# A recommender tower on one core: four slots for the vectors, lookups of chunk 1 ahead of the products of chunk 0, and each step of products in two visits

## The reference

```
e = jnp.stack([tbl_0[ids[:, 0]], tbl_1[ids[:, 1]],
...
combined = jnp.concatenate([dense_features[:, None, :], sparse_features], axis=1)
interactions = jnp.einsum('bnd,bmd->bnm', combined, combined)
interactions_flat = interactions[:, _TRIU_I, _TRIU_J]
...
h = jnp.concatenate([z, r_dense_features], axis=1)
h = jnp.maximum(h @ W_top1 + b_top1, 0.0)
h = jnp.maximum(h @ W_top2 + b_top2, 0.0)
y = h @ W_top3
```

## Time and profile before

| what | value |
|---|---|
| time, median of 3 runs | 372.38 us (370.5 to 372.94) |
| profiled execution, span from first to last instruction | 373.1 us |
| TensorE busy | 332.0 us (89%) |
| GpSimd busy | 258.6 us (69%) |
| VectorE busy, ScalarE busy | 207.1 us, 188.8 us |
| granted TensorE clock, mean | 0.977 |

### The profile page before, as it was taken

How to read it: one execution, slowest core, us unless ns; L and a number is a source line. 1 busy time by engine, 2 the same in 40 slices (tenths; PEclk the granted TensorE clock), 3 DMA queues, 4 the chain that set the end, 5 groups by cost and what they waited for, 6 DMA issues and landing times.

```text
span 373.1 us, 13491 instructions
## 1 busy us (share of the span) xinstructions
PE 332.0 (89%) x6048; PEld 298.5 (80%) x6048; DVE 207.1 (55%) x375; ACT 188.8 (51%) x223; POOL 258.6 (69%) x280
## 2 busy tenths in 40 slices
PE   0377859899999899998999999999999999999895
PEld 0377848898799778996789978998799878997685
DVE  3799745694089703874059912885079704860030
ACT  2698462455545473553635564554645563556402
POOL 6777777777777777777777777777777777776000
PEclk9997898899999999998999999999999999999999
DMA  7999426772226622464215722464226622442230
GB/s 178 246 259 212 135 79 174 193 229 69 55 68 151 198 53 59 95 194 125 58 54 128 233 54 58 93 192 131 58 59 150 205 54 57 105 116 62 51 40 21
DMA packets 49332, 44.24 MB, mean 119 GB/s; under 512 B 33359, under 2 KB 39094, under 8 KB 49274
## 3 DMA queue, kind: packets, MB, share of 16 engines
q1 hardware_dynamic: 39166, 25.36, 26.9%
q0 software_dynamic: 8704, 17.84, 18.2%
q10 hardware_dynamic: 1404, 0.17, 0.3%
HBM read 37.91 MB, written 5.44 MB: 116 GB/s over the span
## 4 chain that ended last, share of the span: by engine, by line
PE 82%; DMA 5%; issue 5%; ACT 4%; DVE 2%; SPq 1%; ACTq 1%; DVEq 0%
PE banks L443 38%; PE banks L462 14%; PE mlp L481 13%; PE moved L426 8%; PE mlp L491 7%; DMA w_sb<-in_tbl_dram 3%; DVE masks L672 1%; ACT vectors L818 1%; ACT hidden L846 1%; PE mlp L502 1%; SPq L250 1%; ACTq L229 1%; DMA scratch<-products 1%; DMA features<-scratch 1%; DVE low L659 1%
## 5 line engine op out<-in xcount | busy, mean ns | idle before, releaser
L401 POOL DMA_INDIRECT rows<-in_tbl_dram,ids_sb x272 | 257.7, 948 | 84.0 <-issue 80.8
L672 DVE TENSOR_TENSOR masks<-hot_ids,row_of 125x512 fp32r<-125x512 int32 (+1 forms) x336 | 185.6, 619 | 93.7 <-PE banks L443 84.8
L443 PE MATMUL banks<-masks,high 125*128 125x256 f32 x592 | 154.3, 298 | 17.4 <-DVE low L659 17.4
L443 PE MATMUL banks<-masks,low 125*128 125x256 f32 x592 | 150.3, 291 | 0.0
L443 PEld LDWEIGHTS banks<-masks,high 125*128 125x128 f32 x592 | 118.9, 201 | 18.1 <-issue 15.2
L443 PEld LDWEIGHTS banks<-masks,low 125*128 125x128 f32 x592 | 119.1, 201 | 0.0
L818 ACT ACTIVATE vectors<-moved 128x512 f32<-128x512 f32 (+1 forms) x80 | 86.8, 1085 | 4.6 <-PE moved L426 4.3
L801 ACT ACTIVATE vectors<-banks 128x512 f32<-128x512 f32 (+1 forms) x40 | 44.4, 1111 | 77.4 <-PE banks L443 77.4
L462 PEld LDWEIGHTS banks<-vectors 128*27 128x27 f32 x4096 | 44.5, 104 | 24.7 <-issue 19.6
L462 PE MATMUL banks<-vectors 128*27 128x27 f32 x4096 | 54.1, 193 | 9.7 <-issue 5.0
L481 PE MATMUL mlp<-features,w_sb 117*128 117x256 f32 x224 | 54.6, 388 | 0.0
(11 more groups left out here) (46 smaller groups left out, 64.4 us busy)
## 6 DMA issues: line engine op xcount, KB each, us to landing
hot_ids<-in_ids_of_field_dram SPq DMA_DIRECT2D x32, 256.0 KB, 4.9
rows<-in_tbl_dram,ids_sb POOLq DMA_INDIRECT x272
features<-scratch SPq DMA_DIRECT2D x7, 351.0 KB
scratch<-products SPq DMA_DIRECT2D x56, 42.2 KB
scratch<-products SPq DMA_DIRECT2D x28, 81.2 KB
w_sb<-in_tbl_dram SPq DMA_DIRECT2D x3, 448.0 KB
hot_ids<-in_ids_of_field_dram SPq DMA_DIRECT2D x8, 128.0 KB
dense_sb<-in_dense_dram SPq DMA_DIRECT2D x8, 128.0 KB, 5.2
```

The costliest lines, as they stand in the source:

```text
L401: pool.indirect_dma_start(rows[:, (tile * TILE_ROWS + v) % RING, :], None, tables[f][:, :], bass.IndirectOffsetOnAxis(ap=ids_sb[:, tile, f ...
L443: last = nc.tensor.matmul(banks[:, j % BANKS, m * CHUNK:(m + 1) * CHUNK], part[:, part_of(j * PAIR + m, k), :], masks[:, mask % MASK_RING, ...
L672: nc.vector.tensor_tensor(masks[:, mask % MASK_RING, 0:size], hot_ids[0:PART_ROWS, n % ID_RING, 0:size], row_of[0:PART_ROWS, row:row + 1]. ...
```

## The change

`TILE_SLOTS` goes from 3 to 4, so that the slots of chunk c+1 are never those of chunk c; the waits for free slots move one tile back, the staging of three tables moves to the fourth slot, and `place_dense(1)` has no wait for steps any more. A step of products is issued in two visits of 8 groups (32 samples, 128 queue instructions), with other work between them: in `end_of_chunk(i)` parts of the first layer, turns and parts of `look_up(i + 1, 0)`. Before chunk 1, `look_up(1, 0)` and most of `look_up(1, 1)` stand ahead of or between the products of chunk 0, steps 2 and 3 of chunk 0 move behind `turn(2, 0)`, and `BANK_OF_FIRST_STEPS` puts the four steps of chunk 0 into banks 0, 2, 3 and 1.

```diff
-TILE_SLOTS = 3
+TILE_SLOTS = 4
+VISITS = 2
+VISIT_GROUPS = STEP_GROUPS // VISITS
+BANK_OF_FIRST_STEPS = (0, 2, 3, 1)
...
+            def multiply(c, s, visits=range(VISITS)):
+                for visit in visits:
+                    multiply_part(c, s, visit)
+
+            def multiply_part(c, s, visit):
+                if c == 0 and visit == 0 and bank_of(c, s) < 2:
+
+                    pe.wait_ge(pair_kept, HOT_PAIRS + bank_of(c, s) + 1)
+                if s == 0 and visit == 0:
                     pe.wait_ge(batch_kept, c * CHUNK_BATCHES + TILE_BATCHES)
...
                 turn(1, 1)
-                multiply(0, 0)
+                look_up(1, 0, range(0, 3))
                 turn(1, 2)
-                multiply(0, 1)
+                look_up(1, 0, range(3, 6))
                 turn(1, 3)
+                look_up(1, 0, range(6, PARTS[0]))
                 turn(1, 4)
-                multiply(0, 2)
-                look_up(1, 0)
-                multiply(0, 3)
+                multiply(0, 0, (0,))
+                look_up(1, 1, range(0, 2))
+                multiply(0, 0, (1,))
+                look_up(1, 1, range(2, 4))
+                multiply(0, 1, (0,))
+                look_up(1, 1, range(4, 6))
+                multiply(0, 1, (1,))
+                look_up(1, 1, range(6, PARTS[1]))
...
                 turn(2, 0)
-                look_up(1, 1)
+                multiply(0, 2, (0,))
+                look_up(1, 2, range(0, 2))
+                multiply(0, 2, (1,))
+                look_up(1, 2, range(2, 4))
+                multiply(0, 3, (0,))
+                look_up(1, 2, range(4, 6))
+                multiply(0, 3, (1,))
+                look_up(1, 2, range(6, PARTS[2]))
                 turn(2, 1)
-                look_up(1, 2)
+                look_up(1, 3)
                 turn(2, 2)
-                look_up(1, 3)
+                look_up(1, 4)
                 turn(2, 3)
-                look_up(1, 4)
                 turn(2, 4)
...
                 b = TILES * i + 1
                 first_layer(i - 1, 0)
-                multiply(i, 0)
+                multiply(i, 0, (0,))
                 turn(b, 0)
                 first_layer(i - 1, 1)
-                multiply(i, 1)
+                multiply(i, 0, (1,))
                 turn(b, 1)
                 first_layer(i - 1, 2)
+                multiply(i, 1, (0,))
                 turn(b, 2)
                 first_layer(i - 1, 3)
                 turn(b, 3)
+                multiply(i, 1, (1,))
                 second_layer(i - 1, 0)
                 turn(b, 4)
                 if i < LAST:
                     second_layer(i - 1, 1)
-                    multiply(i, 2)
-                    look_up(i + 1, 0)
-                    multiply(i, 3)
+                    multiply(i, 2, (0,))
+                    look_up(i + 1, 0, range(0, 3))
+                    multiply(i, 2, (1,))
+                    look_up(i + 1, 0, range(3, 5))
+                    multiply(i, 3, (0,))
+                    look_up(i + 1, 0, range(5, PARTS[0]))
+                    multiply(i, 3, (1,))
```

More of the change, by code:

```diff
@@ L143, in build @@
         w1_again = hidden2[:, :, :].rearrange("p m n -> p (m n)")
-        spare = ((vectors[:, 2 * TILE:3 * TILE, :].rearrange("p s v -> p (s v)"), (0, 1, 8)),
+        spare = ((vectors[:, 3 * TILE:4 * TILE, :].rearrange("p s v -> p (s v)"), (0, 1, 8)),
                  (products[:, :, :].rearrange("p x g -> p (x g)"), (2,)),
@@ L202, in build, with bank_of @@
         CONSTANTS = 4
+        def bank_of(c, s):
+            return s if c else BANK_OF_FIRST_STEPS[s]
         def of_tile(t):
@@ L428, in turn, with look_up @@
                 last.then_inc(batch_ready, 1)
-            def look_up(c, j):
+            def look_up(c, j, ks=None):
+                ks = ks or range(PARTS[j])
                 if c == 0:
                     pe.wait_ge(low_made, PAIR * j + WIDTHS[j])
-                elif j < BANKS:
+                elif c == 1 and ks[0] == 0:
+                    if j == 0:
+                        pe.wait_ge(pair_kept, HOT_PAIRS)
+                    elif j != 1:
+                        pe.wait_ge(step_kept, BANK_OF_FIRST_STEPS.index(j % BANKS) + 1)
+                elif j < BANKS and ks[0] == 0:
                     pe.wait_ge(step_kept, (c - 1) * CHUNK_STEPS + j + 1)
-                if j >= BANKS:
+                if j >= BANKS and ks[0] == 0:
                     pe.wait_ge(pair_kept, c * HOT_PAIRS + j - BANKS + 1)
-                for k in range(PARTS[j]):
+                for k in ks:
                     mask = c * MASKS + FIRST_MASK[j] + k
@@ L453, in multiply @@
                     pe.wait_ge(dense_placed, c + 1)
-                if s == TILE_STEPS:
+                if s == TILE_STEPS and visit == 0:
                     pe.wait_ge(batch_kept, (c + 1) * CHUNK_BATCHES)
                 t, of_step = divmod(s, TILE_STEPS)
-                for g in range(STEP_GROUPS):
+                for g in range(visit * VISIT_GROUPS, (visit + 1) * VISIT_GROUPS):
                     at = of_tile(c * TILES + t) + (of_step * STEP_GROUPS + g) * QUADS
@@ L461, in multiply @@
                         to = q * STRIP
-                        last = nc.tensor.matmul(banks[to:to + VECTORS, s, g * VECTORS:(g + 1) * VECTORS],
+                        last = nc.tensor.matmul(banks[to:to + VECTORS, bank_of(c, s), g * VECTORS:(g + 1) * VECTORS],
                                                 one, one, start=True, stop=True, tile_position=(0, to))
-                last.then_inc(step_ready, 1)
+                if visit == VISITS - 1:
+                    last.then_inc(step_ready, 1)
             def first_layer(c, m):
@@ L483, in first_layer, with second_layer @@
                 last.then_inc(first_ready, 1)
-            def second_layer(c, m):
+            def second_layer(c, m, ks=range(MTILES1)):
                 if c < 0:
@@ L489, in second_layer @@
                     pe.wait_ge(first_kept, MTILES1 * (c + 1))
-                for k in range(MTILES1):
+                for k in ks:
                     last = nc.tensor.matmul(mlp[:, m, 0:CHUNK], w2_sb[:, k, m * 128:(m + 1) * 128], hidden1[:, k, :],
                                             start=(k == 0), stop=(k == MTILES1 - 1))
-                last.then_inc(second_ready, 1)
+                if MTILES1 - 1 in ks:
+                    last.then_inc(second_ready, 1)
             def last_layer(c):
@@ L558, in end @@
                 every = (PAIR_TILES, *range(PAIR_TILES))
-                multiply(LAST, 2)
-                second_layer(LAST - 1, 1)
+                multiply(LAST, 2, (0,))
+                second_layer(LAST - 1, 1, range(0, 2))
+                multiply(LAST, 2, (1,))
+                second_layer(LAST - 1, 1, range(2, MTILES1))
                 multiply(LAST, 3)
@@ L677, in place_dense @@
             def place_dense(c):
-                if c >= 1:
-                    dve.wait_ge(step_ready, (TILES * c - 1) * TILE_STEPS)
+                if c > 1:
+                    dve.wait_ge(step_ready, (TILES * c + TILES - TILE_SLOTS) * TILE_STEPS)
                 dve.wait_ge(dense_loaded[c % 2], 16 * (c // 2 + 1))
@@ L690, in keep_step @@
                     products[0:PRODUCT_ROWS, ::-1, first:first + STEP_GROUPS].rearrange("p x g -> p g x"),
-                    banks[0:PRODUCT_ROWS, s, 0:STEP_GROUPS * VECTORS]
+                    banks[0:PRODUCT_ROWS, bank_of(c, s), 0:STEP_GROUPS * VECTORS]
                     .rearrange("p (g x) -> p g x", g=STEP_GROUPS)).then_inc(step_kept, 1)
@@ L796, in keep_pair @@
             def keep_pair(c, j):
-                if j == 0 and c >= 1:
-                    act.wait_ge(step_ready, (TILES * c - 1) * TILE_STEPS)
+                if j == 0 and c == 1:
+                    act.wait_ge(low_made, HOT)
+                if j == 0 and c > 1:
+                    act.wait_ge(step_ready, (TILES * c + TILES - TILE_SLOTS) * TILE_STEPS)
                 act.wait_ge(mask_used, c * MASKS + FIRST_MASK[j + 1])
@@ L916, in first_chunk @@
                 keep_batch(1, 1)
+                keep_batch(1, 2)
+                keep_batch(1, 3)
+                keep_pair(1, 0)
+                keep_batch(1, 4)
                 keep_step(0, 0)
-                keep_batch(1, 2)
                 keep_step(0, 1)
[L920 to L924, removed]
+                keep_pair(1, 1)
             def second_chunk():
                 keep_batch(2, 0)
-                keep_pair(1, 1)
+                keep_step(0, 2)
+                keep_step(0, 3)
+                keep_pair(1, 2)
                 keep_batch(2, 1)
-                keep_pair(1, 2)
+                keep_pair(1, 3)
                 keep_batch(2, 2)
-                keep_pair(1, 3)
+                keep_pair(1, 4)
                 keep_batch(2, 3)
-                keep_pair(1, 4)
                 keep_batch(2, 4)
@@ L954, in end_of_chunk @@
                 keep_first(i - 1, 0)
-                keep_step(i, 0)
```

(3 more changed lines are left out.)

2 lines of the change are left out of this document (removed).

## The result

The changed kernel takes 377.21 us (median of 4 runs, 376.02 to 377.45), the kernel before in the same comparison 371.44 us (370.31 to 372.94). The ratio is 1.017, with a 95% interval from 1.012 to 1.021: slower by 1.7%, where 371.2 us had been forecast, about no change.

The account below looks back on a forecast made before the run. Gathers and TensorE were taken as nearly equal chains, the gathers limiting TensorE's lead. The span, 373.1 − 2.6 + 1.4 = 371.9, less 0.7 over the median, gave 371.2 us; 8 in 10 range 369.0 to 374.2.

Parts of the forecast that it names:

- The bound: Gathers run without a pause until 343.4 us, nearly as long as TensorE's work, and limit what TensorE can gain.
- The landing: Time for the last batch's gathered rows to arrive before turn(15, 3): taken as 1.5 us, between 0 and 4.2.
- the half clock that was charged at `turn(15, 3)`: TensorE's wait for rows at the last chunk's turn is followed by half clock, costing 1.4 us; likelier than not.
- the late write: write_last(0) moves behind the last turn, to 346.3 from 343.02; TensorE waits 1.8 us, off the path or costing 0.5.
- The size of the base: The profiled span of the kernel before, 373.1 us, was taken as 0.7 over the median time.
- The room ahead of the gathers: At turn(15, 3) TensorE can be ahead by at most 2.7 us, of which 1.8 us can be used.
- The start: In chunk 0, lookups fill waits, but TensorE then waits 5 us for features: +0.6 us, between −2 and +3.
- +3: Two visits: half of the 0.4 us gaps in steps go, less 0.1 us per additional change between kinds of matmul.
- +2: Two visits: shorter stalls for instruction packets at steps of products in the steady part, a gain of about 2 us.
- +2.2: Second layer: half a step now stands before it, so waits for ScalarE's copy shrink, gaining 2.2 us before the last turn.
- +1.4 us: One stretch of TensorE at half clock behind a stall goes in the steady part, a gain of 1.4 us.
- C: Rival: each visit pays for its two changes between kinds of matmul, gaps and packets stay; 379.8 or 376.2 us, chance 0.07.

Follow-up runs that it names:

- e4: The changed kernel without the 17 gathers of tile 2: 372.65 us, ratio 1.001 to the kernel before.
- e9: The changed kernel with the old start, step 1 of the last chunk early, and without the 17 gathers of tile 2: 361.25 us, ratio 0.970.
- e1: The changed kernel with step 1 of the last chunk and its copy moved early: 372.72 us, ratio 1.002 to the kernel before.
- e6: The kernel before with step 1 of the last chunk moved behind turn(15, 3): 379.06 us, ratio 1.018.
- e3: The changed kernel with the old order from the end of chunk 1 on; four slots and the new start stay: 377.18 us, ratio 1.013.
- e7: The changed kernel with the old start and step 1 of the last chunk early: 372.6 us, ratio 1.000 to the kernel before.
- e5: The kernel before without the 17 gathers of tile 2: 369.88 us, ratio 0.994.
- e10: The kernel of e8 measured once more with more rounds: 372.34 us, ratio 1.002 to the kernel before.
- e8: e7 with the last chunk's second layer split around turn(15, 3), and steps 2 and 3 whole in a row: 371.59 us, ratio 0.997.

## Why the prediction was wrong

**The bound was right.** `turn(15, 3)` was forecast at 343.6 and stood at 343.70; the gathers end at 343.4 in both kernels; TensorE's lead turned into waits for rows (e4, e9). The landing, taken as 1.5 us without a row of its own, has one in the chain of the changed kernel: from the start of the fourth batch's last gather (0.94 us long) to the turn, so 1.5 us behind the gather.

```profile
341.19 2.47 DMA rows<-in_tbl_dram,ids_sb
```

Step 3 was forecast to end at 353.5 and ended at 353.88. Without the half clock that was charged at `turn(15, 3)` the forecast span is 373.1 − 2.6 = 370.5 us, and e1, where the late write is put right, spans 371.0.

**The step that failed** is that of `write_last(0)`: "this stays off the path, or costs 0.5". The late write was seen, with its read at 352.7, the features at 355.3 and a wait of 1.8 us. By the forecast's numbers the layers of the first half start at 355.3 and take the 7.8 us that they took before (355.97 to 365.34 − 1.60 = 363.74), so those of the second half start at 363.1, 0.5 behind their features at 362.6. They started at 367.77, 4.7 us later than that. Two terms make it up. The features let TensorE go on 2.05 us later, at 357.35: the 12 writes and their landing took 346.36 to 354.09 = 7.7 us, where 6.4 was taken from the kernel before, and the read took 3.3 us until TensorE went on, where 2.6 was taken. The wait became 3.47 us. And the work behind it took 10.4 us instead of 7.8, 2.65 us more, with the clock at half: the half clock had been charged at `turn(15, 3)` (1.4 us), where the wait came to only 0.8 us and it did not occur, and not behind this longer wait, on the path. So work that had been covered became the end. The edit of this one step is worth 4.5 us in e1 and 6.3 us in e6. How much of that is the late features and how much the clock is read from the traces; no run separates the two.

**The size of the base was off.** The span of the profiled execution was set 0.7 us over the median of the runs. The runs show a time of the span and about 1.9 us. The forecast span of 371.9 would have been a time of 373.8, against which 377.21 is 3.4 off. The rest, 2.6 us, is that the trace of the kernel before came from an execution slower than most. The room ahead of the gathers also differs from execution to execution. In e6 TensorE is ready for `turn(15, 3)` at 342.49 and the rows come at 343.08; with the 1.7 us of step 1 ahead of the turn, as in the kernel before, the room would be 1.1 us and not the 2.7 us read from the one trace. So there may have been less to gain than the 1.8 us counted.

**The start.** Forecast was a wait of 5 us with 1.2 us of half clock behind it, and +0.6 us in all. The changed kernel waited 3.6 us, and its first layer started at 83.67 where 82.5 was forecast; in e3 it started at 86.06, and the start alone cost 5.0 us, some 2.6 of them under the half clock. The mechanism of the wait was right, the total off by 5.6 us. One stall had been left out too. In the changed kernel stands a stall with the cause "issue" that is longer than any of those in the earlier trace rows (1.80 us at most), although the half steps there have lookups between them:

```profile
57.21 0.25 PE L484 MATMUL banks<-vectors 128*27 128x27 f32 x7 [2.38 <-issue]
```

The cost of the start was covered by the waits for the gathers, as e1 and e7 show. That it did not spoil the forecast is in part luck: so costly a start had not been priced, and the lead of the visits was just large enough to take it in.

**Visits and the second layer.** +3, +2, +2.2 and +1.4 us were forecast for them, 8.6 in all up to the last turns; e9 against e5 gives 8.6 us for the whole kernel. A chunk without stalls fell by 0.89 us. The single terms are not told apart by a run, nor are the four slots, so the equality of the two sums confirms their size and not each of them. The Trainium skill's rule in Runtime: NRT & Kernel Launch, section "Instruction fetch mechanics", that fetching is mostly hidden, does not hold in the runs, as it did not in the trace before: stalls of 1.10 and 2.38 us in the changed kernel, and of 2.50 us in e10, stand in steps of short matmuls. That these are waits for the next packet is argued from the places and not shown by a run that changes the fetch: in the kernel before, the two stalls of the last chunk stand 15 + 8 + 105 = 128 matmuls apart, with their weight loads 256 queue instructions. The first of them is this, the second stands above at 355.67.

```profile
351.94 0.31 PE L462 MATMUL banks<-vectors 128*27 128x27 f32 x15 [0.80 <-issue]
```

**The rivals.** None of them was the mechanism. C had the sign and lies near in time, but by a loss to changes between kinds in every chunk. e7 and e9 keep these changes from the end of chunk 1 on and have no loss. The case that came stood as a side remark of the forecast, at its right place, priced at 0.5 us at most and not made a rival.

## What to carry to other kernels

Where two engines run for nearly the same time, a lead of one is worth only what the other leaves, so look for the last instruction of each that the other needs, and keep everything that does not need it ahead of that point. Here one half step whose result starts a chain of writes and reads slid behind such a point and cost 4.5 us, where all the rest of the change together gained nothing that could be measured (e1, e7). When a transfer chain moves, price the wait at its far end together with the half clock that follows it, and compare that sum, not the wait, with the slack. Here it was 3.47 + 2.65 = 6.1 us, against 2.1 us of lead and 1.6 us of idle time: 2.4 us too much.

## What the runs showed that was not expected

TensorE stalled with the cause "issue" in or at its steps of short matmuls for 0.2 to 2.5 us, at the same place in the queue for very different times: at the end of the last step for 0.50 us in the kernel before, 1.10 in the changed one, 1.52 in e1 and 2.50 in e10. Lookups between half steps did not prevent 2.38 us at 54.8 us. e8 and e10 are the same code: in e8's trace the last step stalls 2.26 us and the granted clock is 0.53 from 353.5 to 356.0 us, in e10's it stalls 2.50 us and the clock stays at 1.00. The half clock lasted from 3.4 us (before, at 67 us) to 10.2 us (e3, of which 3.9 us were still the wait).

The 12 writes of the last chunk's first half took 6.4 us to the read behind them in the three kernels whose end has the old order (before, e3 and e5), and 6.6 (e10) to 8.3 us (e4) in the nine others, among them 7.7 in the changed kernel, 8.1 in e6 and 7.7 in e1. What lengthens them was not tried, but the 6.4 us belonged to the old order, and taking them over was part of the error.
